# A Macaron block (experts, attention, experts): attention output with tokens on partitions, and parts of layer 1's router moved into the last attention steps

## The reference

```python
x = x + 0.5 * moe(layernorm(x), router_w, w1, v1, w2)   # layer 0
x = x + attention(layernorm(x), Wq, bq, Wk, bk, Wv, bv, Wo, bo)
x = x + 0.5 * moe(layernorm(x), router_w, w1, v1, w2)   # layer 1, same weights
```

## Time and profile before

| | |
|---|---|
| runs, us | 667.88, 665.50, 663.27 (median 665.5) |
| profiled execution | 667.9, its span in the profile 666.0 |
| busy over the span | PE 626.7 (94%), PEld 525.8, DVE 498.3 (75%), ACT 391.1 (59%), POOL 52.4 |
| layer 0 | 0 to 90 us |
| attention | 90 to 569 us, blocks of 116 to 119 us |
| layer 1 | 569 to 666 us |

### The profile page before, as it was taken

One profiled execution on the slowest core, in us unless ns is written; L12 is line 12 of the kernel. 1 busy time (PEld: TensorE's weight loads), 2 busy tenths in 40 slices (PEclk: granted clock), 3 DMA queues, 4 the chain that ended last, 5 costly groups with the idle time before them and its releaser, 6 DMA issues.

```text
span 666.0 us, 11671 instructions
## 1 busy us (share of the span) xinstructions
PE 626.7 (94%) x4320; PEld 525.8 (79%) x4320; DVE 498.3 (75%) x1309; ACT 391.1 (59%) x1053; POOL 52.4 (8%) x75
## 2 busy tenths in 40 slices
PE   8589999999999999999999999999999999887995
PEld 6367677999888888888888888888888888665774
DVE  6746668889988677887777788876778877773663
ACT  5634475767666566566556666666666656662441
POOL 3443000000000000000000000000000000134210
PEclk9689999999999999999999999999999999969998
DMA  8999940000000000000000000000000034266991
GB/s 318 341 416 419 376 153 1 2 1 1 0 1 1 1 1 0 1 1 1 0 1 1 1 0 1 1 1 0 1 1 2 0 127 190 110 207 228 419 376 48
DMA packets 27619, 62.50 MB, mean 94 GB/s; under 512 B 7014, under 2 KB 17382, under 8 KB 27558
## 3 DMA queue, kind: packets, MB, share of 16 engines
q1 hardware_dynamic: 25398, 55.97, 22.2%
q0 software_dynamic: 1664, 5.30, 2.1%
q10 hardware_dynamic: 496, 0.43, 0.3%
HBM read 54.34 MB, written 7.34 MB: 93 GB/s over the span
## 4 chain that ended last, share of the span: by engine, by line
PE 72%; DVE 12%; ACT 6%; DMA 6%; issue 2%; POOL 1%; SPq 0%; POOLq 0%; DVEq 0%; ACTq 0%
PE bank L1406 18%; PE bank L1408 17%; PE bank L1407 17%; PE bank L1462 7%; PE bank L1217 3%; DMA slots<-token_table,slot_index 3%; DMA down_r<-down_in 3%; PE bank L1257 2%; ACT probs L728 2%; PE bank L1225 2%; PE bank L1267 2%; ACT probsT_hi L739 1%; DVE q_lo L1073 1%; ACT q_hi L711 1%; DVE probsT_lo L1129 1%
## 5 line engine op out<-in xcount | busy, mean ns | idle before, releaser
L728 ACT ACTIVATE probs<-bank,negmax 128x256 f32<-128x256 f32 x256 | 121.4, 494 | 1.8 <-DVE negmax L1087 1.6
L739 ACT CAST probsT_hi<-bank 128x512 fp32r<-128x512 f32 x128 | 68.8, 590 | 70.9 <-PE bank L1462 70.9
L711 ACT ACTIVATE o_hi<-bank,bv 128x512 fp32r<-128x512 f32 x64 | 44.1, 690 | 69.2 <-PE bank L1408 69.2
L1129 DVE TENSOR_TENSOR probsT_lo<-bank,probsT_hi 128x512 fp32r<-128x512 f32 x128 | 81.7, 679 | 0.4 <-ACT probsT_hi L739 0.4
L1087 DVE TENSOR_REDUCE negmax<-bank 128x2 f32<-128x512 f32 x128 | 81.7, 679 | 0.0
L1095 DVE TENSOR_SCALAR probs<-probs,rowinv 128x256 f32<-128x256 f32 x256 | 73.0, 348 | 2.3
L1073 DVE SCALAR_TENSOR_TENSOR o_lo<-bank,bv,o_hi 128x512 fp32r<-128x512 f32 x64 | 48.0, 749 | 34.5 <-ACT o_hi L711 34.5
L1408 PE MATMUL bank<-k_hi,q_lo 128*128 128x256 f32 x256 | 72.4, 283 | 0.0
L1407 PE MATMUL bank<-k_lo,q_hi 128*128 128x256 f32 x256 | 72.3, 283 | 0.0
L1406 PE MATMUL bank<-k_hi,q_hi 128*128 128x256 f32 x256 | 72.2, 282 | 0.0
L1073 DVE SCALAR_TENSOR_TENSOR q_lo<-bank,bq,q_hi 128x512 fp32r<-128x512 f32 x64 | 47.9, 748 | 32.2 <-ACT q_hi L711 31.9
(11 more groups left out here) (184 smaller groups left out, 1294.9 us busy)
## 6 DMA issues: line engine op xcount, KB each, us to landing
up_r<-up_in SPq DMA_DIRECT2D x16, 768.0 KB, 9.3
down_r<-down_in SPq DMA_DIRECT2D x14, 512.0 KB, 11.1
up_q<-up_in SPq DMA_DIRECT2D x8, 768.0 KB, 8.8
up_o<-up_in SPq DMA_DIRECT2D x6, 768.0 KB, 14.6
down_q<-down_in SPq DMA_DIRECT2D x8, 512.0 KB, 9.6
token_table<-xn SPq DMA_DIRECT2D x16, 256.0 KB, 2.4
down_o<-down_in SPq DMA_DIRECT2D x6, 512.0 KB, 16.3
x<-x_in SPq DMA_DIRECT2D x4, 512.0 KB, 5.5
```

Of the source, the lines that this page charges most:

```text
L711: nc.scalar.activation(dst, src, ACT.Identity, bias=bias).then_inc(work_high, 1)
L728: nc.scalar.activation(probs[:, n % 2, t, :], scores_ps[head][:, qt * S:qt * S + S], ACT.Exp, bias=negmax[:, n % 2, t:t + 1], accum_out=ro ...
L739: nc.scalar.copy(probsT[0][:, head].rearrange("p c s -> p (c s)"), probsT_ps[head][:]).then_inc(probsT_high, 1)
L1129: nc.vector.tensor_tensor(probsT[1][:, head].rearrange("p c s -> p (c s)"), probsT_ps[head][:], probsT[0][:, head].rearrange("p c s -> p ( ...
```

## The change

- **Output.** `out_ps[bb]` now has tokens on partitions, one bank for each batch entry: o is stationary, wo moves, 256 columns, twelve matmuls in every step, for step n - 1 in step n. `output_of_pair`, `yT`, its transposes and the copy are gone; o has two homes in place of four.
- **Bias and addition.** bo is spread once, in layer 0, to a row on all partitions (two ACT operations, two matmuls, one copy). VectorE adds it to x in steps 13 and 14 of block 0, 4 and 8 of the others, and adds the bank in step 15 (bb 0) and in step 1 of the next block (bb 1).
- **Chores.** The last statistics operation of a block moves from step 9 to step 10. The moments of tiles 0 to 11 run in steps 11 and 12 of the last block.
- **Layer 1's router.** Token transposes 0 and 1 in step 14, 2 and 3 and expert product 0 in step 15; masks 0 without chores, the last addition and statistics inside masks 1, moments inside masks 2 and 3. The wide token sums come before the codes, the narrow ones behind, then filler of 12 in place of 16.
- **DMA queue.** In layer 1, SP waits for four gathers in place of two before it loads group 6. In layer 0, it waits for group 15's load before it issues the attention weights.
- **First fills.** The low halves 7, 8 and 9 of the weights are made one or two fills earlier.

```diff
-                for n in range(2):
+                for n in range(IN_FLIGHT - 1):
                     sp.wait_ge(gathered[n], 16 * (layer * len(range(n, GROUPS, RING)) + 1))
...
+            sp.wait_ge(home(0, GROUPS - 1)[2], 16 * loads_before(0, GROUPS - 1))
             sp.wait_ge(down_done, done_with_q)
...
-            in_fill = {1: 3, 2: 4, 3: 5, 4: 6, 6: 7, 7: 8, 8: 9}
+            in_fill = {1: [3], 2: [4], 3: [5], 4: [6, 7], 5: [8], 6: [9]}
...
-        SPREAD_AT = (5, 6, 7, 9)
+        SPREAD_AT = (5, 6, 7, 10)
+        BIAS_AT = ((13, 14), (4, 8))
...
+            def add_bias(i, bb):
+                xa = x[:, 4 * i + 2 * bb:4 * i + 2 * bb + 2, :]
+                nc.vector.tensor_tensor(xa, xa, bo_row[:].unsqueeze(1).to_broadcast([P, 2, D]), ALU.add).then_inc(bias_added, 1)
+            def add_output(i, bb):
+                dve.wait_ge(y_raw, y_seen.add())
+                dve.wait_ge(bias_added, 2 * i + bb + 1)
+                xa = x[:, 4 * i + 2 * bb:4 * i + 2 * bb + 2, :].rearrange("p t d -> p (t d)")
+                nc.vector.tensor_tensor(xa, xa, out_ps[bb][:], ALU.add).then_inc(out_added, 1)
...
+                if i is not None and n in BIAS_AT[i > 0]:
+                    add_bias(i, BIAS_AT[i > 0].index(n))
+                if i is not None and n == 15:
+                    add_output(i, 0)
+                if i is not None and i > 0 and n == 1:
+                    add_output(i - 1, 1)
+                take_low(*[t[:, n % 2, :, :] for t in o], bv[:, kv:kv + 1])
...
+                if last and n in (11, 12):
+                    for moment in steps_of_last[6 * (n - 11):6 * (n - 11) + 6]:
+                        moment()
...
+            masks(1, 0)
+            masks(1, 1, [lambda: None, last_output, lambda: spread_of(BLOCKS - 1, 2), lambda: tie(spread_of(BLOCKS - 1, 3))])
             steps = moment_steps(TILES - 4, TILES)
-            masks(1, 1, steps[:7])
-            masks(1, 2, steps[7:])
+            masks(1, 2, steps[:7])
+            masks(1, 3, steps[7:])
...
+                if layer == 0:
+                    take_tokens()
+                else:
+                    take_narrow_tokens()
+                    keep_busy(12)
...
+                for qt in halves:
                     for head in range(2):
+                        h = G * kv + 2 * hp + head
+                        last = three(out_ps[bb][:, qt * D:qt * D + D], [a[:, n % 2, head, qt * P:qt * P + P] for a in o],
+                                     [a[:, h, :] for a in wo], hp == kv == qt == head == 0,
+                                     n in (13, 15) and qt == head == 1, shared=True)
```

More of the change, by code:

```diff
@@ L663, in expert_layer @@
                 warm(ACT.Silu)
+                if layer == 0:
+                    act.wait_ge(bo_crossed, 1)
+                    nc.scalar.copy(bo_row[:], bank[5][:, D:2 * D]).then_inc(bo_ready, 1)
                 act.wait_ge(slotsT_raw, sT_seen.add())
@@ L730, in exps_of, with step @@
                                          accum_out=rowsum[:, n % 2, t:t + 1]).then_inc(exp_ready, 1)
-            def take_output(d):
-                nc.scalar.activation(yT[:, d, :], out_ps[d][:], ACT.Identity, bias=bo[:, d:d + 1]).then_inc(yT_ready, 1)
-            def step(n, i=0, last=False):
+            def step(n, last=False):
                 kv, bb, hp = place(n)
@@ L1159, in _ @@
                     normalise_probs(0)
-                if n in in_fill:
-                    split_low(in_fill[n])
+                for m in in_fill.get(n, []):
+                    split_low(m)
             step(0)
@@ L1340, in expert_layer @@
                 last.then_inc(codes_raw, 1)
-                take_tokens(layer)
-                if layer == 1:
-                    keep_busy(16)
+                if layer == 0:
+                    pe.wait_ge(bo_spread, KD)
+                    for kd in range(KD):
+                        last = mm(bank[5][:, D + kd * P:D + kd * P + P], bo_row[:, kd * P:kd * P + P], ident[:], start=True, stop=True)
+                    last.then_inc(bo_crossed, 1)
+                if layer == 0:
+                    take_tokens()
+                else:
+                    take_narrow_tokens()
+                    keep_busy(12)
                 pe.wait_ge(first_ready, keys_seen.add())
@@ L1526, in step @@
                 if last and n == STEPS - 1:
-                    for u in range(2):
+                    for u in range(2, 4):
                         transpose_tokens(1, u)
+                if n == 12 and jobs:
+                    project(*jobs.pop(0))
+                    output_product(n - 1, i, [0])
+                ahead = 2 if n == STEPS else 1
                 for m, job in enumerate(jobs):
@@ L1545, in step @@
                 last_use[("o", n % STEPS)] = uses[0]
+                if last and n == STEPS - 2:
+                    pe.wait_ge(exp_ready, exp_seen.add(4))
+                    for u in range(2):
+                        transpose_tokens(1, u)
             xn4_seen.add(4)
```

184 lines of the change are left out of this document (58 added, 126 removed).

## The result

| | before | after |
|---|---|---|
| median, us | 667.5 (7 runs) | 658.4 (7 runs, 657.55 to 662.54) |
| ratio of the runs | | 0.9902, 95% interval 0.9875 to 0.9930 |
| profiled execution, its span | 667.9, 666.0 | 658.05, 656.2 |

The account below looks back on a forecast made before the run. TensorE was taken to bound the attention, and a chain of waits through VectorE's masks, filler matmuls and one gather the part after. Terms summed to -14.2 us, from 665.5 to 651.3 us, range 646.5 to 657.5.

Parts of the forecast that it names:

- The small matmuls: Attention output product: twelve small matmuls for six large cost 0.09 us per step in 48 products, +4.3 us.
- steps 2 and 3: Attention blocks 1 to 3: without transposed outputs, six steps each lose 1.16 us, -7.0 us.
- step 10: Attention, two blocks: a statistics operation moved here from step 9 removes VectorE's lateness of 0.42 us, -0.8 us.
- the moments: Steps 11 and 12 of the last block: 14 small operations at 0.166 us are a new stall, +2.3 us.
- the last step to the codes: Transposes of step 15 to second code product: reordered transposes and VectorE work save 2.3 us.
- weight load: Attention output matmuls, two rivals: loads fully exposed, 701 us, chance 0.04; a third exposed, 665.1 us, chance 0.05.
- the wait for group 15's load: End of layer 0: competing bytes go, so TensorE's 0.81 us wait for that load goes, -0.8 us.
- The first fills: Start of attention: low halves of wo made earlier, away from the chain to k_lo, -1.0 us.
- the codes to the slot keys: Layer 1's router: wide sums before the codes and less filler let TensorE take the keys sooner, -4.7 us.
- the four gathers: Layer 1's first slots: gathers land before weight loads start, so TensorE starts sooner, -4.4 us.
- the clock's: Rival, router part: TensorE's clock stays low over filler and narrow sums, 654 to 656.5 us, chance 0.14.
- the gathers are not freed: Rival, layer 1's first slots: the gather change does not work, 4.4 us comes back, 655.7 us, chance 0.12.

Follow-up runs that it names:

- the two runs above: Changed kernel plus 16 tiny unused ScalarE activations in layer 1, four gathers: 660.96 us; kernel before with only the wait for four gathers: 663.64 us.
- the changed cast: Changed kernel with VectorE's cast of the ranks to int32 replaced by a multiplication by 1.0: 657.38 us.
- both parts undone: Changed kernel without the wait for group 15's load and with moments of tiles 0 to 11 back in the first masks: 653.96 and 652.85 us.

## Why the prediction was partly right

**Right.** The small matmuls cost 0.09 us in q steps, steps 2 and 3 fell from 7.60 to 6.53, step 10 lost 0.34, the moments cost 2.3, the last step to the codes came out at 18.53 for a forecast of 18.6. No weight load showed beyond these 0.09 us. The attention as a whole was better than the sum by 1.95 us, for two reasons that the forecast did not have: step 16 went from 9.71 to 9.26 in three blocks (I had +0.09 each, so 1.6 of it; its inside I have not taken apart), and the two products moved out of the last block's steps 11 and 12 saved 2.11, for 1.75 that they cost in steps 13 and 14 of block 0. That these gave 2 us is luck, not foresight.

**Wrong: the wait for group 15's load** (forecast -0.8, measured +2.05 by ten profiles against six). The step that failed is that the wait brings a gain of 0.8 because "the competing bytes go", with the late start put aside: "their arrival limits the first projections only if wo, last in the queue, comes more than a microsecond or two after ACT wants it, an end of +1". It was the case, since wo landed 3.5 us later than without the wait and ACT stood for 1.83 us at it. And the "only" was wrong: ACT stood for 1.62 us at wk, the first in the queue, and the projection of k came 2.3 us late before wo was wanted. I had counted the bytes that no longer compete and not the time in which nothing moves: before, the transfers are issued from 62.67 on and stand ready behind the experts' loads, so the queue never runs dry; with the wait the issue starts at 78.28, and 75 to 80 moves 77 GB/s, where it moves 297 without the wait. And I took the 0.81 us of one row for the price of the old order, where further profiles have 0 to 0.2. ScalarE took k_hi only behind the high part of wo (96.10 behind 95.56), so a late wo holds up k_hi, which does not need it. The first fills did gain (step 0 to step 1, 9.33 to 8.56, -0.77 for a forecast of -1.0).

**Wrong: the codes to the slot keys** (-4.7 against -3.4). Of the 1.3 us, 0.8 are the end that I had named, narrow sums at the lower clock: 5.7 us for 4.1, and between 4.3 and 7.1 in the other profiles. TensorE was 0.8 us late in this one and 1.0 to 1.2 in seven others; in six others VectorE is last, 10.95 us behind the codes. The other 0.5 us are VectorE's. The step that failed is that its 9.3 us carry over (10.4 from the start of the second code product). They end with the cast, and the cast ends with GpSimd's product, before the change and after it. That product ends 0.52 us later behind the codes than it did, since ScalarE's exponentials start 0.53 later; the cast starts 0.46 us earlier and gains nothing. I had read the cast's 0.25 us as its price, and it was only what was left of the wait.

The Trainium skill has a rule for this, which the prediction did not use: "SBUF — State Buffer", SBUF: two separate sides, says that VectorE and GpSimd share a pair of ports as an exclusive lock, for VectorE operations in a two-port mode or with two inputs in SBUF (these only against a GpSimd operation that reads SBUF), and that whichever starts first keeps it for its whole instruction while the other blocks. The trace agrees in the length of the wait, with 1.21 to 1.25 us for cast, tensor-scalar and scalar-tensor-tensor forms, the length of one GpSimd instruction, and 0.43 for the max beside the same product. No run here shows which mode the cast and the tensor-scalar form use.

**Wrong in its net: the four gathers** (-4.4 against -1.27). The mechanism is as forecast where ScalarE does not stall: 4.7 us in the kernel before, 12.3 to 12.7 us from keys to fourth up product. Two things took the gain. ScalarE's stall of 3.1 us stands in the same place, and with it the late gathers are covered anyway; its cause is open, and the forecast could not have had it from the profile before. And where it is absent, up to 2.2 us come back at slots 13 to 15: 1.4 and 2.2 in the two runs above, 1.6 without the filler, 0.7 with the changed cast, and 0 to 0.9 in the three kernels with both parts undone. For this the forecast had the sentence "group 6 is wanted only six slot steps in" and looked no further: the loads run at 380 to 430 GB/s nearly without a gap from their start to about 636 us (about 644 in the two runs above), so a later start is a later end, whichever group is asked for first. Whether the end is late enough to be waited for differs from one profile to the next, and what decides it was not tested.

As to the rivals: the clock's (654 to 656.5) happened, at 0.8 us; "the gathers are not freed" did not happen in its own terms but in its price. The result lies above the range because one term of -0.8 was about +2, for which I had an end of +1, and because clock, GpSimd and slots fell short in the same run; the better attention made good a part. The miss is 0.9 us at the range's upper bound, which is within what the median of a repeat moves by: of the two repeats one lies outside (659.66) and one inside (657.22, beside a kernel before at 668.22).

## What to carry to other kernels

A wait put before a DMA issue is priced by the time in which the queue then runs dry and by every transfer behind it, the first one too, not by the bytes that no longer compete. Where a stream of loads runs without a gap to the end, a gain at its head that delays the stream can be lent: look at the last slots for what comes back. And when an operation of VectorE moves in time, look at what GpSimd does at its new place, and ask when GpSimd ends, not how long the operation took before.

## What the runs showed of the hardware

- VectorE's first elementwise operation on [128, 32] took 1.21 to 1.25 us beside GpSimd's tensor-tensor product and ended within 0.05 us of that product's end, in three forms; the next one, with GpSimd idle, took 0.17. Max and match-replace took 0.43 and 0.41 beside the same product.
- The same program has a stall of ScalarE of 1.3 to 3.5 us in one place on two chips and none on a third. A packet of 8192 bytes on an instruction queue goes by at that time on all of them, so it does not explain the stall by itself. The Trainium skill ("Runtime: NRT & Kernel Launch", Instruction fetch mechanics) calls the cost of crossing from one block of instructions to the next mostly hidden; these runs neither show a case against it nor clear it.
- A gather alone took 2.9 us; beside loads the fifth took 7.2 us from issue to landing, as the 7.3 of the earlier trace rows, and freeing the gathers brought the fourth up product 4.7 us forward in the kernel before. The rule of the Trainium skill that the prediction weighed ("DMA: Bandwidth & Descriptors", Queues, rings and completion order), was read there as a gather that waits only for its turns and loses little; the runs bear out the trace and not that reading.
- Sixteen matmuls of 16 rows and 256 columns took between 3.9 and 7.1 us from one profile to another, with the granted clock over them between 0.94 and 0.51.
